# The order of TensorE's side work inside the opening of a two-layer block

## The reference

```python
x = L0_attn_x                                            # (2, 1024, 512)
mod = (_silu(L0_c) @ L0_wmod).reshape(2, 6, 1, -1)       # six rows of 512 for each batch item
sa, ca, ga, sb, cb, gb = ...
h = _layernorm(x, axis=-1) * (1 + ca) + sa
q = _rmsnorm(h @ wq_a.T, q_a_ln_w) @ wq_b.T              # 32 heads of 64 + 64
ckv, k_pe = split(h @ wkv_a.T)                           # 32 latent numbers and 64 rotated ones
kv = _rmsnorm(ckv, kv_a_ln_w) @ wkv_b.T                  # the nope part of the keys, and v, per head
...
out = attn @ v  ->  out @ wo.T
```

## Time and profile before

| what | us |
|---|---|
| median of 3 runs | 2172.82 (2171.63 to 2172.96) |
| the profiled execution's own time | 2168.36 |
| its span, first to last instruction | 2166.6 |
| TensorE busy in the span | 1990.0 |
| the opening | 0 to 126.2 |

### The profile page before, as it was taken

The page is one execution under the profiler, slowest core; times in us unless marked ns, Lnnn a source line. Parts: engine busy times, 40 slices in busy tenths (PEclk is TensorE's granted clock), DMA queues, the critical chain, the costliest instruction groups (busy, mean ns, idle before and its releaser), DMA issues. The chain is left out here.

```text
span 2166.6 us, 34181 instructions
## 1 busy us (share of the span) xinstructions
PE 1990.0 (92%) x12648; PEld 1151.5 (53%) x12648; DVE 1161.2 (54%) x2541; ACT 885.1 (41%) x1877; POOL 480.5 (22%) x376
## 2 busy tenths in 40 slices
PE   5859999999999999999967999988999999999698
PEld 4535666666666666666634454544444444444244
DVE  3536655555555555555402445437667667663166
ACT  3413344444444444444431222222666666666222
POOL 0014245555444444455330000000000000000000
PEclk8869999999999999999988999995999999998799
DMA  9742233222233323332135211153223212211201
GB/s 311 263 143 59 60 79 80 66 59 56 68 80 80 79 70 80 79 80 62 39 119 179 73 63 48 60 132 93 42 33 52 47 33 52 47 18 27 89 29 49
DMA packets 113592, 172.19 MB, mean 79 GB/s; under 512 B 26186, under 2 KB 46826, under 8 KB 113298
## 3 DMA queue, kind: packets, MB, share of 16 engines
q1 hardware_dynamic: 112402, 169.75, 29.7%
q10 hardware_dynamic: 1024, 0.26, 0.1%
HBM read 84.32 MB, written 29.38 MB: 52 GB/s over the span
## 5 line engine op out<-in xcount | busy, mean ns | idle before, releaser
L886 ACT ACTIVATE at_prob<-at_scp 128x512 f32<-128x512 f32 (+1 forms) x608 | 349.8, 576 | 515.5 <-PE at_scp L989 514.3
L1659 ACT ACTIVATE as_prob<-as_scp 128x512 f32<-128x512 f32 (+2 forms) x640 | 309.0, 563 | 200.2 <-PE as_scp L1755 148.9
L921 DVE CUSTOM_DVE_ANT_0 at_junk<-at_mxp,causal 128x128 f32<-128x128 f32 (+3 forms) x512 | 243.6, 488 | 189.9 <-PE at_mxp L1000 185.2
L1709 DVE TENSOR_REDUCE as_mxd<-as_mxp 128x2 f32<-128x256 f32 (+3 forms) x256 | 203.5, 821 | 98.3 <-PE as_mxp L1774 96.0
L916 DVE TENSOR_REDUCE at_mxf<-at_mxp 128x1 f32<-128x512 f32 x256 | 176.1, 688 | 142.7 <-PE at_mxp L1000 138.9
L1694 POOL TENSOR_TENSOR l_att_t<-l_att_t,as_spread 64x1024 f32<-64x1024 f32 x16 | 37.9, 2367 | 861.5 <-DMA as_spread<-l_recips 861.5
L1707 DVE TENSOR_REDUCE as_mxf<-as_mxp 128x2 f32<-128x1024 f32 x128 | 151.0, 1221 | 60.3 <-PE as_mxp L1769 60.1
L816 POOL TENSOR_TENSOR at_pre<-at_prob 128x512 f32<-128x512 f32 x64 | 80.2, 1282 | 409.8 <-ACT at_prob L886 409.8
L816 POOL TENSOR_TENSOR at_pre<-at_pre,at_prob 128x512 f32<-128x512 f32 x128 | 160.6, 1285 | 3.6 <-ACT at_prob L886 1.2
L1793 PE MATMUL as_op<-as_prob,l_vn 128*32 128x512 f32 (+3 forms) x1536 | 160.4, 540 | 0.0
L985 PE MATMUL at_scp<-hd_early_q,l_khi 97*128 97x512 f32 (+1 forms) x304 | 138.1, 454 | 10.9 <-DMA hd_late_q<-at_slo 8.2
(11 more groups left out here) (232 smaller groups left out, 3352.8 us busy)
## 6 DMA issues: line engine op xcount, KB each, us to landing
hd_late_q<-at_slo SPq DMA_DIRECT2D x96, 128.0 KB, 2.4
at_qhi<-at_shi SPq DMA_DIRECT2D x96, 128.0 KB, 2.4
at_qlo<-at_slo SPq DMA_DIRECT2D x96, 128.0 KB, 2.4
hd_early_q<-at_shi SPq DMA_DIRECT2D x84, 128.0 KB, 2.5
at_spread<-l_recips SPq DMA_DIRECT2D x64, 128.0 KB, 2.8
l_o<-at_u_sb SPq DMA_DIRECT2D x16, 512.0 KB, 3.3
hd_early<-in_wmod SPq DMA_DIRECT2D x7, 1024.0 KB, 7.8
hd_late<-l_o SPq DMA_DIRECT2D x12, 512.0 KB, 4.4
```

The costliest lines, as they stand in the source:

```text
L886: nc.scalar.activation(prob[:, x % RING0, c0:HALF], scp[x % BANKS0][:, c0:HALF], ACT.Exp).then_inc(s["exp_done"], 1)
L921: nc.vector.tensor_tensor_reduce(out=junk[:, u % 2, 0:w], in0=tile[:, 0:w], in1=k.causal[:, HALF - w:HALF], scale=1.0, scalar=LOWEST, op0= ...
L1659: nc.scalar.activation(prob[:, x % RING1, cols], scp[x % BANKS1][:, cols], ACT.Exp).then_inc(s["exp_done"], 1)
L1709: nc.vector.reduce_max(mxd[:, t % 2, :, i, qt:qt + 1], tile[:, :, 0:(qt % 4 + 1) * P], AX_X).then_inc(s["mx_done"], 1)
```

## The change

The `FILL` table becomes a list of lists: for each half, for each of its four tiles, the pieces of side work. In the second and third half the first tile has two joined groups, the second and the third tile one each, the fourth tile none. The first and fourth half have what they had. In the second to fourth half TensorE does the first tile's pieces ahead of the first product, behind the transposes of the first two tiles; the first half keeps its order. ScalarE's copies follow the same table and stay behind `modulated`.

```diff
-FILL = [[("lat",)], [("vo", g) for g in range(4)], [("vo", g) for g in range(4, 8)], [("rows", 0, 1), ("cols", 0, 1), ("rows", 0, 2), ("g",)]]
+FILL = [[[("lat",)], [], [], []], [[("vo", 0), ("vo", 1)], [("vo", 2)], [("vo", 3)], []], [[("vo", 4), ("vo", 5)], [("vo", 6)], [("vo", 7)], []],
+        [[("rows", 0, 1)], [("cols", 0, 1)], [("rows", 0, 2)], [("g",)]]]
 TAIL = [("d", c) for c in range(C)] + [("rows", 1, 2), ("rows", 1, 0), ("cols", 1, 0), ("rows", 1, 1), ("cols", 1, 1)]
-WPLACES = [("rows", 0, 0), ("cols", 0, 0)] + [place for what in sum(FILL, []) + TAIL
+WPLACES = [("rows", 0, 0), ("cols", 0, 0)] + [place for what in sum(sum(FILL, []), []) + TAIL
                                               for place in ([("lat", 0), ("lat", 1)] if what == ("lat",) else [what])]
@@ TensorE, half(g)
                     for i in range(TH):
                         if i + 1 < TH:
                             normed(first + i + 1)
+                        ahead = g > 0 and i == 0
+                        for what in work[i] if ahead else ():
+                            fill(what)
                         products(first + i)
-                        for what in work[i:i + 1]:
+                        for what in () if ahead else work[i]:
                             fill(what)
@@ ScalarE, half(g)
-                        for what in work[i:i + 1]:
+                        for what in work[i]:
                             copied(what)
```

## The result

Over 20 runs each, the changed kernel takes 2162.58 us (2160.3 to 2170.61) and the kernel before 2172.06 (2167.3 to 2174.82). The ratio is 0.9966 [0.9958, 0.9975], that is 7.4 us faster [5.4, 9.1]; 4.0 were forecast. The ratio goes by the means, 2163.9 and 2171.3; the medians are further apart, 9.5 us. The span of the profiled execution fell by 6.4 us, 2166.6 to 2160.2.

The account below looks back on a forecast made before the run. TensorE was taken to bound most of the kernel, a ring over engines the opening. Work and order -1.1, clock -2.5 and rest -0.4 made -4.0 us: 2168.8 us from 2172.8, range 2163.8 to 2174.5.

Parts of the forecast that it names:

- The second half: Second half: groups 0 and 1 wait for L540, 1.8 us, and one more group precedes the deviation, 1.0: +2.8 us.
- The order in the third and fourth half: Side work moved into the pauses: -1.0 us in the third half with -0.5 for ScalarE's copy, -1.9 in the fourth.
- ScalarE's copy: Second and third half: no group's copy between ScalarE's squares any more, -0.5 us each, -1.0 in all.
- The clock: Second to fourth half: 8.9 us at the lower clock level for 13.9, -2.5 us, between -6.0 and +1.0.
- the middle: Third and fourth half: 2.5 and 2.7 us at the lower level, between clock held (0) and fallen (5.0, 5.5).
- The rest: Opening behind the fourth half: moved as a whole, with its clock able to win 5 us or lose about 2; -0.4.
- moved as a whole: Behind the opening's barrier: runs as before, so the opening's gain or loss goes one for one into the time.
- the clock staying high: Rival, third and fourth half: no fall of the clock there, -8.1 us in all, 2164.7 us; chance 0.20.
- no difference: Whole kernel: time within 0.2%, 4.3 us, of the kernel before; chance 0.46.
- The wait and the clock take it all: Rival, opening: only the parts without the clock win, -1.1 us, 2171.7 us; chance 0.16.
- slower: Rival, second to fourth half: joined groups don't bring the clock up, +5.2 us, 2178.0 us; chance 0.10.
- the rule on transposes: Ahead of the pauses: transposes don't count as busy, so groups behind them break the gap and the clock holds, -8.1 us.

Follow-up runs that it names:

- second_only: The change in the second half only, other halves as in the kernel before: 1.7 us slower than the kernel before, ratio 1.0008 [0.9998, 1.0018].
- scaled_early: Changed kernel with VectorE's two L540 instructions moved ahead of the second half's normalising: 10.0 us faster than the kernel before, ratio 0.9954.
- third_only: The change in the third half only, other halves as in the kernel before: 8.0 us faster than the kernel before, ratio 0.9963.
- third_fourth: The change in the third and fourth half only, second half as in the kernel before: 7.8 us faster than the kernel before, ratio 0.9964.
- fourth_only: The change in the fourth half only, other halves as in the kernel before: 3.0 us faster than the kernel before, ratio 0.9986.
- work_twice: Kernel before, with matmuls that are computed again later added in the third and fourth half's pauses: 5.0 us faster than the kernel before, ratio 0.9977.

## Why the prediction was right, and where not

**The second half.** Right in mechanism and size: the groups wait for L540, 1.9 us behind the first modulated tile, and the half grew by 1.9 in second_only and 3.1 in the changed kernel, for +2.8 - 0.5 forecast, and more or less clock. The trace of scaled_early shows that the wait is the cause. With 0.4 us that the opening was late already ahead of this half, the third half's first product came at 67.74, where near 66 was forecast.

**The order in the third and fourth half.** Forecast -1.5 and -1.9. At the high level they measure 17.60 - 15.98 = 1.6 and 11.46 - 9.43 = 2.0. ScalarE's copy gave 3.29 - 2.81 = 0.5, as worked out.

**The clock.** Forecast -2.5 over three halves, with "the middle" for each of two pauses of "about 2 us"; they were 2.8. The prediction took them as 4.03 less the work moved in, and left out that a half in the new order has no group behind its last product, so that TensorE reaches the next pause sooner: in second_only the pause behind the new half is 0.66 longer (4.69), and 4.70 in third_only, with nothing moved into either. In the profiled execution the clock held behind one and fell behind the other: 2.4 won in the third half, 14.08 - 10.96 - 2.0 = 1.1 in the fourth, about 0.8 lost in the second: -2.7. That this meets the -2.5 is in part luck. The middle stood for two outcomes of which each pause has one or the other, and another execution can have both high or both low.

**The rest.** -0.4 forecast, 26.68 - 27.94 = -1.3 in the profiled execution, where the modulation rows ran at the high level sooner. That the change does this isn't shown: with the same new order in the fourth half the rest took 28.2 us in third_fourth and 29.5 in fourth_only. The profiled opening is 5.0 us shorter, for 4.0 (+3.1, -4.0, -3.1 and -1.3, and 0.4 more ahead of the second half, each rounded).

**What follows the opening** was put at "moved as a whole". It took 1.5 us less in the profiled execution (2040.3 to 2038.8), and that is no effect of the change that could be shown: over the twelve kernels it lies between 2037.5 and 2043.7 with the same instructions.

**The sum.** 7.4 us by the runs, against -4.0, is inside the range, though the median of its own runs, 2162.6, lies 1.2 below the lower end. It isn't in the band of the forecast (-2 to -6.5, 0.54), but in the one given to the clock staying high (-6.5 to -10, 0.20). The clock alone was worth 5.0 us [3.0, 7.0] in work_twice, where I had 2.5 for the clock in the halves and 0.4 for the rest. So the clock is the term that may have been too small, and with it the chance of 0.46 for "no difference" too large; but work_twice left pauses of 2.2 us and not of 2.8, and for the changed kernel itself it isn't shown. The rival that the clock stays high in both halves (the prediction calls it the third) forecast 0.7 us more than was measured, the forecast 3.4 less; its sum has 3.9 us at the lower level for the second half, where the text gives 3.7, which is 0.1 us. Its mechanism isn't what the traces show: of the five pauses of 2.8 us in them, the level held behind one. How the 7.4 divide over executions, which a single trace can't show, stays open. So does why third_only alone came out as fast as the whole change; what fits is that it has neither the wait in the second half nor a pause of 2.84 us ahead of the third, but one of 2.18, behind which the clock held.

**The rivals.** "The wait and the clock take it all" and "slower" fell: the first is out by the interval of the 7.4 us, and in second_only the product right behind the two groups took 1.78 us, the high level, so the clock did come up while joined groups ran. In the changed kernel the 3.57 us in which they ran stayed at 0.50, and it rose some 2 us later. Of the rule on transposes (the Trainium skill, "TensorE: Matmul & The Clock Gate", "Part 4: PE-mode transpose") no run here decides. What the prediction made of it, groups that break the gap in two and keep the level high, isn't borne out: behind one pause of 2.84 us that followed groups the clock held, behind another it fell.

## What to carry to other kernels

Side work belongs in the pause ahead of a waited-for product, if all that it waits for is ready there: look for the release of its buffers on the other engines first, since whatever stands behind it in the list waits too. Price the clock beside the work: here a pause cut from 4 to 2 us was worth at least as much by the clock (2.4 and 2.6 us) as by the work moved (1.6 and 2.0). When the pause is a ring over several engines, find the small instruction on which it turns; one square root moved by one place gave 4.5 us more than the changed kernel.

## What the runs showed of the hardware

Whether the clock fell behind a pause went with its length here: behind all pauses of 2.2 us or less ahead of a first product it stayed at 2.4 GHz (thirteen, in eight kernels), behind those of 4.0 to 4.7 it fell each time (eleven, in six kernels). In between it went either way: it held behind 2.36, fell during the product behind 2.44 (twice), and of five of 2.81 to 2.84 it held behind one, for the same instructions.

Transposes follow the level too: those of L362 and L363 start 0.11 us apart from 102.1 us on in the kernel before, and 0.21 to 0.22 apart from 111.7 us on, behind the d products at the lower level.

The same instructions don't take the same time in every execution. The second half's first product, ahead of which all kernels with the old order there run the same list, starts at 45.04, 45.05 and 45.09 in three, and at 46.97 and 47.70 in two others; in the last, third_only, the 64 small matmuls of L285 had taken 7.04 us, for 5.82 in the kernel before. The column of the granted clock doesn't tell why: it reads 1.00 from 27.2 to 34.3 us there, against 0.62 from 26.9 to 33 in the kernel before. The median of the kernel before moved between 2169.7 and 2172.5 us over four series of 11 to 21 runs; this scatter and that of 6 us in "later" would explain it, but three of the series ran on three different chips, and no run separates the two. So effects of 2 us have to be read in a trace's own stretches.
